# Attention in a decoder layer: maxima for eight heads at once, and longer distances between the stages

## The reference, cut to what matters

```python
x = layernorm(x + attention(x))            # scores = q k / 4 + alibi bias; softmax; weights times v; out projection
x = layernorm(x + cross_attention(ctx, x)) # the same with k and v from ctx (120 rows) and a mask
x = layernorm(x + experts(x))              # top 2 of 8 experts, 256 -> 1024 -> 256
```

## Time and profile before

| | us |
|---|---|
| median of 3 runs | 1415.66 (1412.86 to 1416.01) |
| the profiled execution, its own time | 1412.27 |
| its span in the profile | 1410.2 |
| PE busy | 1091.7 (77%) |
| DVE busy | 1022.0 (72%) |
| ACT busy | 567.4 (40%) |
| POOL busy | 483.5 (34%) |
| bytes moved by DMA | 202.20 MB |

### The profile page before, as it was taken

One profiled execution on the slowest core, in us unless ns is written; L12 is line 12 of the kernel. 1 busy time (PEld: TensorE's weight loads), 2 busy tenths in 40 slices (PEclk: granted clock), 3 DMA queues, 4 the chain that ended last, 5 costly groups with the idle time before them and its releaser, 6 DMA issues. The chain is left out here.

```text
span 1410.2 us, 32514 instructions
## 1 busy us (share of the span) xinstructions
PE 1091.7 (77%) x9874; PEld 772.1 (55%) x9875; DVE 1022.0 (72%) x2410; ACT 567.4 (40%) x1022; POOL 483.5 (34%) x597
## 2 busy tenths in 40 slices
PE   3778899889888888888885600088999999999980
PEld 2445666666655655565553400066777777777750
DVE  2579999999888989999985340066777777777764
ACT  1344555555545656665563200022323323332324
POOL 1233433433344343534322037612223223223324
PEclk7799999999999999999997555599999999999995
DMA  8489886678756887788754152275222222222227
GB/s 207 108 225 226 230 200 142 157 180 227 174 108 163 235 237 154 207 232 221 202 168 137 68 194 106 100 267 159 42 43 43 41 45 41 41 45 41 43 30 245
DMA packets 160383, 202.20 MB, mean 143 GB/s; under 512 B 30444, under 2 KB 141692, under 8 KB 157067
## 3 DMA queue, kind: packets, MB, share of 16 engines
q1 hardware_dynamic: 145864, 182.92, 48.7%
q0 software_dynamic: 13296, 17.83, 7.5%
q10 hardware_dynamic: 1152, 0.53, 0.2%
HBM read 122.63 MB, written 74.41 MB: 140 GB/s over the span
## 5 line engine op out<-in xcount | busy, mean ns | idle before, releaser
L1177 PE MATMUL HB<-xhi,W 128*128 128x128 f16 x2272 | 292.1, 221 | 21.7 <-issue 16.1
L1177 PEld LDWEIGHTS HB<-xhi,W 128*128 x2272 | 202.2, 98 | 65.8 <-issue 48.2
L1177 PE MATMUL HB<-xlo,W 128*128 128x128 f16 x1136 | 225.0, 220 | 0.0
L1460 POOL DMA_INDIRECT d_sums<-ysc,tok x71 | 111.0, 1563 | 327.3 <-DMA XB<-d_rows 171.7
L892 ACT ACTIVATE PT<-SB 128x1024 f32<-128x1024 f32 x128 | 131.1, 1024 | 138.3 <-PE SB L563 136.3
L659 DVE TENSOR_REDUCE mneg<-SA 128x4 f32<-128x1024 f32 x128 | 156.5, 1223 | 41.6 <-PE SA L515 39.5
L1177 PEld LDWEIGHTS HB<-xlo,W 128*128 x1136 | 111.9, 99 | 50.2 <-issue 0.7
L1370 DVE SCALAR_TENSOR_TENSOR hlo<-HB,hhi 128x512 f16<-128x512 f32 x142 | 98.2, 691 | 55.1 <-ACT hhi L1238 51.1
L1238 ACT ACTIVATE hhi<-HB 128x512 f16<-128x512 f32 x142 | 84.2, 593 | 121.3 <-DVE HB L1362 121.2
L1362 DVE SCALAR_TENSOR_TENSOR HB<-HB,SC,b1c 128x512 f32<-128x512 f32 x142 | 107.1, 754 | 16.7 <-PE HB L1177 11.9
L1246 ACT ACTIVATE ysc<-yb,wv 128x256 f32<-128x256 f32 x71 | 36.1, 508 | 191.8 <-DVE yb L1394 181.6
(11 more groups left out here) (195 smaller groups left out, 2500.4 us busy)
## 6 DMA issues: line engine op xcount, KB each, us to landing
wst<-in_w SPq DMA_DIRECT2D x32, 1024.0 KB, 10.0
d_w<-w SPq DMA_DIRECT2D x16, 1024.0 KB, 6.7
W<-d_w SPq DMA_DIRECT2D x8, 2048.0 KB, 8.7
k_stack<-d_k SPq DMA_DIRECT2D x96, 128.0 KB, 7.2
XB<-d_rows SPq DMA_DIRECT2D x71, 130.0 KB
d_rows<-fill SPq DMA_DIRECT2D x4, 1950.0 KB, 15.6
d_q<-q_part SPq DMA_DIRECT2D x16, 384.0 KB, 5.8
d_k<-k_part SPq DMA_DIRECT2D x16, 384.0 KB, 2.7
```

Of the source, the lines that this page charges most:

```text
L1177: mm = pe.matmul(out, w.rearrange("p e n -> p (e n)"), x[n % 2][:, k, :], start=(k == 0 and half == 0 and x is xhi), stop=(k == KT - 1 and ...
L1460: pool.indirect_dma_start(YS, bass.IndirectOffsetOnAxis(ap=tok[n % 6][:, 0:1], axis=0), ysc[n % 2][:, :], None, compute_op=ALU.add).then_i ...
```

## The change

What it does, part by part:

- The cross attention in units 4 to 7 of step i is that of batch i - 2, not i - 1 (CROSS = 2); the program runs two more steps, to B + 3, and step 3 is written out rather than looped.
- Transposed scores and exponential are three units back, not one (KEYED); weighing four, not two (WEIGHED); turning and dividing five, not three (TURNED).
- split_maxima() runs in each second unit, for the eight heads of two groups; so do the turn in maxima(), and the copy and the spread into the q stack, now in a function spread() of its own. The parts of the maxima take 24 rows of the stack in place of 12 (AUX 27, not 15). divide() does the division on its own.
- The stacks are read in halves of eight heads, each with its own semaphore, each when its half is free and waited for by the units that use it. A half of q or k takes 3 transfers; those of k read a part once and write it to one, two or three blocks.
- GAPS and ITEMS are new: O and AOT come in the next step's units 1 and 0, Q in unit 2, K and T1 in 3, Vc in 4, Oc in 5, Qc in 6, Kc and V in 7; late() runs in units 3 and 7, not 0 and 5. The order of SyncE's and GpSimd's step is new with them. x1bo has four buffers, the context two (cT, cTv).

```diff
-AUX = 15
 PARTS = 3
+AUX = PARTS + PARTS * GM          # GM = 8 heads
+KEYED, WEIGHED, TURNED = 3, 4, 5
+CROSS = 2
-K_BLOCKS = [0, 0, 0, 1, 1, 2]
+K_RUNS = [(0, 0, 3), (3, 1, 2), (5, 2, 1)]
...
-    GAPS = {(0, 0): ("Q", 1), (0, 1): ("T1", -1), (1, 0): ("Qc", -1), (2, 0): ("Vc", -1),
-            (2, 1): ("AOTc", -2), (3, 0): ("K", 1), (3, 1): ("Oc", -2), (4, 1): ("Kc", 0),
-            (5, 1): ("V", 1), (6, 0): ("T2", -2), (6, 1): ("AOT", 0), (7, 0): ("O", 0), (7, 1): ("R", -2)}
+    GAPS = {(0, 0): ("T2", -4), (0, 1): ("AOT", -1), (1, 0): ("O", -1), (1, 1): ("R", -4), (2, 0): ("Q", 1),
+            (3, 0): ("K", 1), (3, 1): ("T1", -1), (4, 0): ("Vc", -2), (4, 1): ("AOTc", -3), (5, 0): ("Oc", -3),
+            (6, 0): ("Qc", -1), (7, 0): ("Kc", -1), (7, 1): ("V", 1)}
...
+        def read_stack(n, b, k):
+            wait(sp, f"wr_{n}", (b + 1) * 16)
+            for block0, part0, count in (Q_RUNS if n in ("q", "cq") else K_RUNS):
+                dst = stack[n][block0 * HD:(block0 + count) * HD, k * HM:(k + 1) * HM, :].rearrange("p m t -> p (m t)")
...
+                    src = dpart[n][k, part0].rearrange("(d m) t -> d (m t)", m=HM)
+                    src = src.unsqueeze(0).to_broadcast([count, HD, HM * width[n]])
+                sp.dma_start(dst, src).then_inc(sem(f"st_{n}{k}"), 16)
...
         def step(i, mode):                              # SyncE
+            if on(i + 1) and not (isinstance(i, int) and i < 0):
+                wait(sp, "V", i + 1)
+                (xT of batch i + 1 in)
             experts_in(i - 1, mode, 1)
+            if on(i - 2):
+                load_context(cTv, i - 2, "Vc", "ld_cTv")
+                write_parts("ck", i - 2)
+            if on(i - 1):
+                load_context(cT, i - 1, "Kc", "ld_cT")
             (x of batch i in; x2 of batch i - 4 out, in two transfers)
+            if on(i - 2):
+                for k in range(KT):
+                    wait_apart(sp, "STc", NG * (i - 2) - 2 + 2 * k, "wr_mask", 16)
+                    read_stack("ck", i - 2, k)
+                    read_mask(i - 2, k)
+                    read_stack("cq", i - 2, k)
             if on(i + 1):
                 write_parts("q", i + 1)
+                write_parts("k", i + 1)
+            experts_out(i - 1, mode, 0)
             if on(i + 1):
+                wait_apart(sp, "ST", 2 * NG * i + NG, "wr_mask", 16)
+                read_stack("q", i + 1, 0)
+                read_stack("k", i + 1, 0)
             (weights in: experts_in(i, mode, 0))
+            if on(i + 1):
+                wait_apart(sp, "ST", 2 * NG * (i + 1), "wr_mask", 16)
+                read_stack("q", i + 1, 1)
+                read_stack("k", i + 1, 1)
+            if on(i - 1):
+                write_parts("cq", i - 1)
             if isinstance(i, int) and i < 0:
                 later_loads()
             experts_out(i - 1, mode, 1)
             fill_rows(i)
...
+        def divide(u, i):                               # VectorE
+            mine, b, g = group(u, i, TURNED)
...
+            chain(dve.reciprocal(rc[:, :, :], turned[:, :, :, HD]))
...
+        def spread(u, i):
+            mine, b, g = group(u, i, 2)
+            if u % 2 or not on(b):
+                return
+            wait(dve, f"MT{c}", KT * b + d + 1)
+            dve.tensor_copy(mts[0:AUX, :], MT[0:AUX, 0:L]).then_inc(sem(f"mcopy{c}"), 1)
+            wait(dve, f"mcopy{c}", KT * b + d + 1)
+            dve.tensor_copy(stack[q][PROD:PROD + AUX, GM * d:GM * d + GM, :],
+                            mts[0:AUX, :].unsqueeze(1).to_broadcast([AUX, GM, L])).then_inc(sem(f"aux{c}"), 1)
...
         def split_maxima(u, i):
             mine, b, g = group(u, i, 0)
+            if u % 2 == 0 or not on(b):
+                return
...
         def step(i, mode):                              # GpSimd
+            deviations("", i - 1)
             split("q", i + 1)
-            split("cq", i - 1)
+            (x1bo of batch i - 1)
             split("k", i + 1)
-            deviations("c", i - 2)
-            (x1bo of batch i - 1)
-            split("ck", i)
             (xbo of batch i)
-            deviations("", i)
+            deviations("c", i - 3)
+            split("cq", i - 1)
+            split("ck", i - 1)
```

More of the change, by code:

```diff
@@ L224, in iterations @@
         step(-1, None)
-        for i in (0, 1, 2):
+        for i in (0, 1, 2, 3):
             step(i, "max")
-        looped(step, eng, 3, 6, "max", chain, per)
-        step(6, "max")
+        looped(step, eng, 4, 7, "max", chain, per)
         step(7, "max")
@@ L235, in iterations @@
         step(B, "halve")
-        step(B + 1, None)
+        for i in (B + 1, B + 2, B + 3):
+            step(i, None)
     def looped(step, eng, first, end, mode, chain, per):
@@ L483, in item @@
             elif name in ("O", "Oc"):
+                if isinstance(i, int) and i <= 1:
+                    wait(pe, "ld_w2", 80)
                 wait(pe, "read_AOT" if name == "O" else "read_AOTc", b + 1)
@@ L537, in maxima @@
         def maxima(u, i):
-            mine, b, g = group(u, i, 1)
-            if not on(b):
+            mine, b, g = group(u, i, 2)
+            if u % 2 or not on(b):
                 return
             c = "" if mine else "c"
-            wait(pe, f"mparts{c}", NG * b + g + 1)
-            last(pe, u, i, 2, "mcopy")
+            wait(pe, f"mparts{c}", KT * b + g // 2 + 1)
+            mine2, b2, g2 = group(u, i, 4)
+            if on(b2):
+                wait(pe, "mcopy" if mine2 else "mcopyc", KT * b2 + g2 // 2 + 1)
             for t in range(QT):
@@ L621, in step @@
                 gap(u, 0, i)
+                maxima(u, i)
                 scores(u, 1, i)
@@ L698, in split_maxima @@
         def split_maxima(u, i):
             mine, b, g = group(u, i, 0)
+            if u % 2 == 0 or not on(b):
+                return
             c = "" if mine else "c"
-            p0, p1, p2 = (MTp[:, :, 3 + GH * a:3 + GH * (a + 1)] for a in range(PARTS))
-            if on(b):
-                wait(dve, f"max{c}", (2 if mine else 1) * (NG * b + g + 1))
-                chain.put(dve.tensor_copy(p0, mneg[:, :, :]))
-            if on(b):
-                chain.wait()
-                chain.put(dve.tensor_tensor(mr[:, :, :], mneg[:, :, :], p0, ALU.subtract))
@@ L709, in split_maxima @@
-            gap(u, 0, i)
-            if on(b):
-                chain.wait()
-                chain(dve.tensor_copy(p1, mr[:, :, :]))
-                dve.tensor_tensor(p2, mr[:, :, :], p1, ALU.subtract).then_inc(sem(f"mparts{c}"), 1)
+            p0, p1, p2 = (MTp[:, :, 3 + GM * a:3 + GM * (a + 1)] for a in range(PARTS))
+            wait(dve, f"max{c}", (2 if mine else 1) * (NG * b + g + 1))
+            chain(dve.tensor_copy(p0, mneg[:, :, :]))
+            chain(dve.tensor_tensor(mr[:, :, :], mneg[:, :, :], p0, ALU.subtract))
@@ L737, in item @@
                 wait(dve, "xbo" if name == "O" else "x1bo", b + 1)
-                dve.tensor_tensor(r1[:, :, :], BK[1][:, :].rearrange("p (t n) -> p t n", n=D),
-                                  (xbo if name == "O" else x1bo)[:, :, :], ALU.add
+                more = xbo[:, :, :] if name == "O" else x1bo[:, bass.ds(b & 3, 1)].rearrange("p s t d -> p (s t) d")
+                dve.tensor_tensor(r1[:, :, :], BK[BANK[name]][:, :].rearrange("p (t n) -> p t n", n=D), more, ALU.add
                                   ).then_inc(sem(f"read_{name}"), 1)
@@ L820, in step @@
                     halves(u, i, mode)
-        iterations(step, dve, chain, 8 * 3 + 8)
+        iterations(step, dve, chain, 8 + 4 * 3)
     @block.scalar
```

224 lines of the change are left out of this document (103 added, 121 removed).

## The result

The changed kernel takes 1475.12 us (median of 4, 1474.86 to 1478.93), the one before 1415.84 in the same session (1412.86 to 1424.59): a ratio of 1.0414, interval 1.0366 to 1.0463. It is slower by 4.1%, 59 us; the forecast was 1367.

The account below looks back on a forecast made before the run. DVE was taken as the bound, with PE taking over after the change. Steps gain 53.9 us, the start 7, the end loses 15: 46 us off 1412.3 makes 1366, given as 1367; range 1343 to 1400.

Parts of the forecast that it names:

- The bound is DVE, with PE 3 us behind: Steps 2 to 6 before the change: VectorE works almost without a break, busy 39.44 of 43.28 us.
- 3.0 us of waits go: TensorE's step: waits for the spread (2.12), parts of the maxima (0.34) and x1 (0.56) vanish, leaving 1.4 us.
- waits only change their name: Rival for the full steps: removed waits return elsewhere, 1.1 us a step gained, 1405 us; chance 0.07.
- The sum on VectorE: VectorE's step: savings on splits, copies, spreads and pauses between instructions make its list 6.5 us shorter.
- the double spreads: VectorE's step: four spreads of double width take 3.0 us in place of 4.38, 1.4 saved (0.5 to 2.2).
- The split: VectorE's step: four of eight splits of the maxima go, saving 3.62 us less 0.1 for wider rows.
- the second rival: Full steps: GpSimd holds VectorE's spreads and splits, so VectorE stays the bound; 2.0 us a step saved, 1392; chance 0.13.
- Start: 7 us gained.: Steps 0 and 1: k stacks arrive some 3 us sooner each with half the bytes ahead; between 0 and 12.
- x for Q: SyncE's step start: x behind 1 MB out, needed about 10 us later, lands in time; costed at nothing.
- The cross stacks come late: Rival in SyncE's step: ck parts and first half stack land late, each step loses some 6 us, 1450; chance 0.12.
- Steps 8 to 14: Step 8 counted at 3.5 us gained; steps 9 to 14 at 4.4 each (1.1 to 5.7), 26.4 together.
- End: 15 us lost.: After step 15: batch 14's cross attention and the deeper pipeline make 82 us of 67; loss between 8 and 22.

Follow-up runs that it names:

- b_ldve: The kernel before the change, with VectorE's weight maxima reading only 8 numbers of each 512; 1411.77 us, one run.
- a_xt_bank: a_xt with K and T1 in exchanged PSUM banks and Oc half a unit away from AOTc; 1445.47 us, one run.
- a_best_four: a_best with the maxima split, turned, copied and spread for four heads at a time again; 1482.11 us, ratio 1.0481.
- a_xt: The changed kernel with x issued at the end of SyncE's step before, ahead of the 1 MB out and the fill; 1450.87 us, ratio 1.0265.
- a_best: The changed kernel with x issued early, SyncE's transfers reordered, and a new gap plan with matching banks and issue orders; 1420.44 us, ratio 1.0038.

## Why the prediction was wrong, point by point

**"The bound is DVE, with PE 3 us behind": the step that failed.** It was read from busy time (39.44 of 43.28) and from the absence of long waits. b_ldve takes 3.5 us from that list and the step stays. 3.5 us off VectorE give nothing, 4.7 off TensorE 1.2, both 1.5; hand-overs between the engines held most of the step, and which of them is open. The change took 4.0 us of busy time off VectorE and 0.9 off TensorE; by the two tests I estimate that this is worth a microsecond or so a step, not 3.5 to 4.4, before anything new is late.

**"3.0 us of waits go", so that 1.4 us of idle time remain on TensorE: the term that failed in the sum.** PE's busy time came out as forecast (37.95 for 37.8), its idle time at 5.4. That TensorE would hold the step came true; its floor had the waits wrong. The waits named did go for 2.5 of it, those for x1s stayed. New ones of 3.4 us came: SA behind the maximum, Oc behind AOTc, Vc behind x1T. I had "waits only change their name" at 0.07 and 1405; for the steady step it was the right case, 43.4 for 43.3. Two of the new waits could be read from the plan: neighbours AOTc and Oc in units 4 and 5, and T1 and Vc in one bank. a_xt_bank shows them paid in full in steps 5 and 6.

**The sum on VectorE, 6.0 us of busy time and 0.5 of pauses.** Measured 4.0 of busy time, with 24 instructions fewer. The copy (1.1) and the double spreads (1.5 for 1.4) came out as counted: the row of one is 685 to 744 ns where I took 620 to 880. The split didn't: four at 1277 ns, so 2.1 us saved and not 3.5. The 0.7 that is still missing is in no other line. Durations of neighbouring instructions overlap, so that they add up to more than the busy time: to 42.4 us a step for 39.4 before, to 37.6 for 35.4 in steps 5 and 6 after. 4.8 us of durations went, and 4.0 of busy time; I had added durations and set them against busy time (steps 5 to 7; count, busy us, mean ns, as in the earlier trace rows).

```profile
L730 DVE TENSOR_TENSOR mr<-mneg,MTp 128x16 f32<-128x16 f32 x12 | 6.0, 498 | 0.4
L732 DVE TENSOR_TENSOR MTp<-mr,MTp 128x16 bf16<-128x16 f32 x12 | 5.0, 419 | 0.4
...
L718 DVE COPY q_stack<-mts 27x2048 bf16<-27x2048 bf16 x6 | 4.5, 744 | 0.2
```

The median of the first is 176 ns; the mean is that of a few that are held. In order of time one such is seen, with GpSimd's instruction beside it, both ending at 334.9:

```profile
333.61 1.27 POOL L1001 TENSOR_TENSOR x1bo<-x1s,rows_b 128x512 f32 x1 [1.02 <-ACT x1s L887]
333.75 1.17 DVE L732 TENSOR_TENSOR MTp<-mr,MTp 128x16 bf16<-128x16 f32 x1
```

The held time didn't halve with the count: (498 - 176 + 419 - 181) x 4 = 2.2 us a step, where before (340 - 168 + 219 - 172) x 8 gives 1.8. That is the second rival's mechanism, at a size that decides nothing in this kernel; in a_best_four, where it holds seven instructions of a step, it does weigh. The rival had 0.85 us for each spread and 0.2 for a two-operand instruction of the split. It was the other way round: the spread for cq takes 685 to 687 ns each time, and what is held are single instructions of the splits, for up to 1.1 us. The Trainium skill (SBUF — State Buffer, "SBUF: two separate sides") names the port that GpSimd and VectorE share as a point of contention; the two rows agree.

**"Start: 7 us gained."** 10.2 us lost up to step 2, 24 up to step 5. The first scores wait for the k stack as before (to 30.3 us, and 3.9 and 2.5 us more in steps 0 and 1), with half the bytes ahead of them. x for Q was costed at nothing, on 10 us of cover against 8.1 us for 1 MB. I named the fill's 8.78 us and gave it no price: PE waited for x up to 6.1 us a step, 19 us in steps 1 to 4 and 14 in 10 to 14. Over the whole kernel that term cost 21 to 24 us by a_xt, of which 6.3 came back up to step 5, since the cross stack was late behind it.

**The cross stacks come late (0.12, 1450).** Hidden behind x in the changed kernel, 22 us of waits once x is early. It was the nearest rival to the time, and the slower side held 0.09 in all.

**Steps 8 to 14.** 26 us gained were counted for steps 9 to 14; measured are 8.8 gained in 8 and 9 and 14.2 lost after them, with the two transfers in the list and a granted clock of 0.94 where the same steps had 0.99 before. Why steps 8 and 9 gain was not looked into.

**"End: 15 us lost."** From the end of step 15 (about 776) to the last router copy it is 95.5 us where 82 were forecast and 67 were before: 28.5 lost. Step 15 itself is 4.4 longer, where 3.0 were to be gained; together the 32.9 of the table. The path was named rightly (Qc in unit 6 of step 16, its transfers, a deeper pipeline) and sized too small. Qc came 29 us into the step and not 20 (804.76), behind 4.6 us of wait for the cross stack of batch 14; from it to the scores were 25 us and not 17.6; only the rest was short, 41.8 for 44.5. With the early Qc of a_best the 32.9 are 16.6; below that nothing tried got.

**The miss, added up.** The forecast was 46 us gained, the traces have 62.6 lost, 108.6 apart: 17.2 up to the start of step 2, 70.4 in steps 2 to 14 (50.9 not gained, 19.5 lost), 21.0 from the start of step 15 on.

No version beats both kernels. The best of the changed design, a_best, ends 0.4% above the kernel before (0.2 to 0.6).

## What to carry to other kernels

Before costing the removal of work from an engine, make that engine lighter in the kernel as it is: one run with shorter operands says whether it holds the step, which a busy share of 91% does not. When a plan of issues is rewritten, walk one step of each queue in order and put every transfer, fills too, behind what stands before it; and walk the compute plan for neighbours where the second takes the first's result or its bank. Here waits that were moved off one place of the engines' ring came back at another, and removing two of them paid in full only in two steps where no transfer was late.

## What the runs showed of the hardware

- The instruction that issues a transfer can hold its queue for long: 12.76 us for a fill, 6.4 us for x behind another, in a kernel where most take 0.4 us each.
- A copy of 2048 bf16 numbers over 27 partitions takes 685 ns at least, of 1024 numbers over 15 partitions 419 ns at least: twice the numbers, 1.6 times the time. The Trainium skill (VectorE: DVE Perf Modes, "The perf-mode tier table") has 693 ns for it, which agrees.
- A subtraction of 16 numbers in a row takes 176 ns where one of 8 takes 168 (medians): at these two sizes the count of instructions is all, except where GpSimd holds them, up to 1.27 us. In a_best_four the casts of 8 numbers take 0.90 to 1.06 us beside such an instruction.
- Durations of VectorE's neighbouring instructions overlap: in a step they add up to 42.4 us for 39.4 of busy time, so that a small one that goes frees less than its duration.
- Waits of 0.6 and 1.1 us on TensorE's list, neither of which looks like much, added up: 1.7 us of them removed gave 1.6 us of step in two steps, and nothing in steps 9 to 14.
